# One drain on TensorE raises the chunk semaphore by two, in layer 1 of a two-layer GNN kernel

## The reference

```python
# layer 0
agg = segment_sum((x @ W_l.T + b_l)[src], dst) ; deg = segment_sum(1, dst)
x = layernorm(x + agg / max(deg, 1) + x @ W_r.T)
# layer 1 (reads the edges the other way round: h[dst] summed at src)
neigh = segment_sum(h[dst] @ W_neigh.T + b_neigh, src) / max(deg, 1)
y = h + relu(h @ W_self.T + b_self + neigh)
x = layernorm(h + layernorm(y) * ln_gamma + ln_beta)
```

## Time and profile before

| | |
|---|---|
| median of 3 runs | 4257.75 us (4251.17 to 4269.38) |
| the profiled execution's own time | 4222.63 us |
| its span | 4220.8 us, 57125 instructions |
| TensorE busy, weight loads | 2795.4 us (66%), 1186.1 us (28%) |
| VectorE busy | 2605.4 us (62%) |
| ScalarE busy | 813.8 us (19%) |
| GpSimd busy | 1896.1 us (45%) |
| DMA, mean over the span | 139 GB/s |

### The profile page before, as it was taken

The page is one execution under the profiler, slowest core; times in us unless marked ns, Lnnn a source line. Parts: engine busy times, 40 slices in busy tenths (PEclk is TensorE's granted clock), DMA queues, the critical chain, the costliest instruction groups (busy, mean ns, idle before and its releaser), DMA issues.

```text
span 4220.8 us, 57125 instructions
## 1 busy us (share of the span) xinstructions
PE 2795.4 (66%) x11308; PEld 1186.1 (28%) x11308; DVE 2605.4 (62%) x6523; ACT 813.8 (19%) x2156; POOL 1896.1 (45%) x2073
## 2 busy tenths in 40 slices
PE   1000088888888888866999655555555555568887
PEld 1000033333333433322554211111111111124443
DVE  3878877777777777754555444444444444448887
ACT  0300044444444444410222000000000000002222
POOL 0600066666666666664000366666666666630000
PEclk9555599999999999976999766666566665669999
DMA  3300066666666666664333566666666666661111
GB/s 141 123 0 0 21 169 165 170 165 167 167 169 166 168 167 167 168 202 137 102 103 98 160 178 173 179 179 179 177 178 174 180 177 177 172 115 60 55 60 50
DMA packets 201222, 586.38 MB, mean 139 GB/s; under 512 B 34672, under 2 KB 35502, under 8 KB 201196
## 3 DMA queue, kind: packets, MB, share of 16 engines
q0 software_dynamic: 148480, 488.56, 42.6%
q1 hardware_dynamic: 52716, 97.53, 7.1%
HBM read 534.51 MB, written 51.44 MB: 139 GB/s over the span
## 4 chain that ended last, share of the span: by engine, by line
PE 38%; DVE 19%; issue 19%; DMA 8%; DVEq 6%; POOL 2%; another core or an unknown queue 2%; ACT 2%; SPq 2%; POOLq 0%; ACTq 0%
PE ps L710 37%; DMA rows<-table,idx_ring 7%; DVEq L576 4%; DVE acc L583 3%; DVE onehot L569 2%; POOL rows L364 2%; DVE flat L501 2%; DVE flat L502 1%; DVE flat L503 1%; DVE where L598 1%; PE ps L812 1%; DVE st L658 1%; DVE spot L596 1%; PE ps L815 1%
## 5 line engine op out<-in xcount | busy, mean ns | idle before, releaser
L364 POOL DMA_INDIRECT rows<-table,idx_ring x1856 | 1793.8, 966 | 1394.7 <-issue 462.6
L710 PE MATMUL ps<-rows,onehot 128*128 128x512 f16 (+1 forms) x5568 | 1393.7, 381 | 758.0 <-DVE onehot L569 346.3
L583 DVE TENSOR_TENSOR acc<-acc,ps 128x513 f32 x928 | 638.2, 688 | 830.5 <-issue 353.7
L710 PE MATMUL ps<-where,put 128*128 128x464 f16 x3328 | 805.5, 365 | 348.8 <-ACT put L859 291.4
L710 PEld LDWEIGHTS ps<-rows,onehot 128*128 128x128 bf16 x5568 | 526.5, 111 | 1650.1 <-issue 888.2
L569 DVE TENSOR_SCALAR onehot<-iota_node,loc_ring,rows 128x128 bf16<-128x128 f16 x1856 | 586.4, 323 | 297.6 <-DMA rows<-table,idx_ring 253.1
L858 ACT ACTIVATE put<-spot,flat 128x128 f16<-128x128 f16 x832 | 334.1, 402 | 1091.7 <-DVE spot L596 860.7
L710 PEld LDWEIGHTS ps<-where,put 128*128 128x128 f16 x3328 | 268.1, 98 | 659.2 <-issue 351.8
L598 DVE TENSOR_SCALAR where<-iota_chunk,hi_ring 128x928 f16<-128x928 f16 x832 | 378.8, 455 | 0.0
L872 ACT ACTIVATE flat<-acc,rdeg 128x512 f32 (+1 forms) x98 | 69.4, 710 | 1551.2 <-DVE rdeg L647 1547.6
L710 PE MATMUL ps<-w_a,flat 128*128 128x512 f32 x784 | 356.0, 597 | 0.1
(11 more groups left out here) (131 smaller groups left out, 1361.9 us busy)
## 6 DMA issues: line engine op xcount, KB each, us to landing
rows<-table,idx_ring POOLq DMA_INDIRECT x1856
table<-rows SPq DMA_DIRECT2D x98, 257.0 KB, 3.2
h_scratch<-rows SPq DMA_DIRECT2D x49, 256.0 KB, 2.0
rows<-h_scratch SPq DMA_DIRECT2D x49, 256.0 KB, 2.7
acc<-in_x SPq DMA_DIRECT2D x4, 3072.0 KB, 23.5
rows<-in_x SPq DMA_DIRECT2D x48, 256.0 KB, 3.2
out<-rows SPq DMA_DIRECT2D x48, 256.0 KB, 2.0
w_a<-in_w_l_t SPq DMA_DIRECT2D x1, 1024.0 KB
```

The lines of the kernel that those rows point to most:

```text
L364: nc.gpsimd.indirect_dma_start(out=rows[:, k % GB, :], out_offset=None, in_=tables[layer][:, :], in_offset=bass.IndirectOffsetOnAxis(ap=id ...
L583: V.tensor_tensor(tile_acc, tile_acc, part, ALU.add).then_inc(s_acc, 1)
L710: return nc.tensor.matmul(*args, skip_group_check=True, **kw)
```

## The change

In layer 1 the count product no longer raises the semaphore. After the last product of each group of two chunks, a drain on TensorE raises `s_mm` by two. Layer 0 keeps its raise by one in each chunk. All waits for `s_mm` stay as they are written.

```diff
-                    mm(ps[:, bank + 1, 0:1], lhs, row[:, 2 * D + 2:2 * D + 4].bitcast(bf16)[:, 0:1],
-                       start=start, stop=stop).then_inc(s_mm, 1)
+                    last = mm(ps[:, bank + 1, 0:1], lhs, row[:, 2 * D + 2:2 * D + 4].bitcast(bf16)[:, 0:1],
+                              start=start, stop=stop)
+                    if layer == 0:
+                        last.then_inc(s_mm, 1)
+                    elif stop:
+                        nc.tensor.drain().then_inc(s_mm, g)
```

## The result

The change costs little: 4272.07 us median (4268.03 to 4278.99) against 4257.34 us for the kernel before (4251.17 to 4269.38), a ratio of 1.0035 (1.0025 to 1.0044). That is 15 us of loss (11 to 19), inside what the prediction called the same, and twice its 7.

A forecast was written before the change was run, and what follows sets the result against it. GpSimd's gathers, at 1.25 us each plus stalls, were taken to set layer 1's pace. Credit 7, drain 0 and raises 0 sum to +7 us, put on the 4257.75 us median: 4265 us, range 4215 to 4330.

The forecast's parts named there:

- The term of the credit: Layer 1's gather ring: odd gathers wait for one chunk more, so half the stalls come one gather earlier; +7 us.
- The cases of 0: Layer 1's stalls: a run of gathers that ends sooner starts the next with less lead, so the price is 0.
- the 14 or the 70: Layer 1's early stops: 14 us if 119 stalls replace 112; upper bound 70 us if stalls keep their end.
- I take 0: TensorE's drains in layer 1: hidden in its 585 us of idle time, so 0 us are added.
- The second rival: Layer 1's drain on TensorE is not hidden and delays the next gather's credit: +63 us, 4321 us; chance 13%.
- The size of one uncovered drain: TensorE in layer 1: 0.17 us of a chunk's uncovered end plus 0.24 us of refill, 0.41 us per drain.
- the 190 us: TensorE's time for 464 drains at 0.41 us each in layer 1, forecast to lie in its idle time.
- the gathers that end a stall: Sign in layer 1's gathers on GpSimd: the one ending a stall would nearly always be odd, counted from 1.
- the broken stream: Sign on TensorE in layer 1: its stream of chunks is broken after each pair, at 0.3 to 0.5 us.
- GpSimd's mean long idle: Sign in layer 1: GpSimd's mean idle in long stalls stays as before, with a few more stalls.
- The third rival: Layer 1's drained raise passes where the matmul's is late, giving longer gather runs: 59 us less, 4199 us; chance 15%.
- The first: Layer 1's slow stretches end by themselves, so each early stop is paid in full: +70 us, 4328 us; chance 15%.

## Why the prediction was right, and where it was not

**Time and sign** were right: 4272 in 4215 to 4330, a loss within 0.5%. The number came out partly by luck, since the 7 us stood on the wrong term. **The term of the credit** was too large, 7 us where 1 and 3 were measured (the intervals reach from -2 to 7). Its counting was right: before the padded end, 93 of 97 stalls of the kernel with pairs and no drain stand in front of an odd gather, against 44 of 91 before. What was too dear is what an early stop costs. The cases of 0 (an early stop is made up for) describe it better than the 14 or the 70.

**The step that failed is "I take 0" for the drain**, "It lies in TensorE's idle time". 464 drains cost 14 to 19 us by themselves, and with the credit's 1 to 3 they make the change's 15, within the intervals. The second rival, "the drain is not hidden", is the one that happened, at a quarter of its price of 63 us, and by its own sign: "many new idles of 0.4 to 1 us in mid-run". The size of one uncovered drain was right (0.47 us measured on a backlog, 0.41 worked out). 15 us is 8% of the 190 us that the drains would cost if all stood on the path.

The mistake in the reasoning was to set the drain against idle time as an average. Much of TensorE's idle time lies in the slow stretches (before, 62 idles above 2.5 us hold 241 of the 585) and not in the backlogs behind them, and there an uncovered drain has nothing to hide in. Each takes most of the lead that TensorE gains on the gathers (0.28 us per pair left of 0.75), so that the credit of the next gathers comes a little late. The short idles in the table fit this in size and place; it is read from profiles, and no run tested it by itself.

The other reading is that the holds of 4.7 us cost the time. They are real: idle times of TensorE above 2.5 us in which VectorE completed two one-hots or more occur in none of the kernels without a drain, and 62 times in the first 1290 us of the stage with the drain alone. But TensorE stood still in slow stretches before as well, GpSimd's long idles did not grow, and the kernel with a drain in each chunk has only 4 such holds and loses most. So the holds are not needed for the loss. That they have no part in it with one drain per group is not shown.

Of the other signs, the gathers that end a stall (147 of 155 odd before the padded end) and the broken stream came as forecast. GpSimd's mean long idle did not stay (1.40 us for 1.9), TensorE's idle time in the stage grew from 585 to 621 us, and the stage's 1409.8 us and layer 0's 1460 can't be compared with the profile before.

**The third rival**, that a drained raise passes where a product's is late, is refuted: the drain ends late itself, GpSimd waited for it as long as it had for products, and no kernel with drains is faster than before. **The first** (stalls that keep their end) is refuted by the kernel with six buffers, 9 us where 2.5 us more for each of 112 stalls would have given 280. The inference that a stall ends 0.6 us after the last rows have landed holds in the price and not in the gaps: after the change the restart at 3157.16 comes 3.47 us after the last gather's start and not 4.1.

**On the pages.** The Trainium skill ("PSUM — Partial Sum Buffer", section "Engine vs sequencer instructions") puts the increment on the producing product for correctness, and says that a drain waits until the engine is fully idle. It gives no price. A drain's row here runs until its group's products are over and at times beyond (by 4.7 us in the one shown), and TensorE starts nothing before it ends, which agrees with the second. The runs add the price: raises by two cost 1 us on the product, and 15 with the drain.

The 12 us that 464 fewer increments would save by the Trainium skill ("TensorE: Matmul & The Clock Gate", section "The cost: per-tile semaphore tail") did not show: the two kernels of layer 1 that differ in that alone measured 1.0003 and 1.0007, 2 us apart with intervals of 4 us either way.

**Open.** What the slow stretches are: the runs show their marks (register instructions of 0.70 us, products' signals and drains that end late), and that they are absent in the one set that ran on the fastest chip. The 434 to 465 us between that chip and the others are most likely their cost. Whether it is the chip or its state at the time can't be told from one set each. What the change costs on a chip without them was not tried, nor a product's length added to each group at an unchanged clock, which would settle how much of the cost is the backlog.

## What to carry to other kernels

Put a raise of a whole group on the group's last product, where its cost could not be told from nothing in layer 1, and keep drains off a stream that others feed: each drain uncovers the end of a product and a refill. Don't cover a cost with an engine's average idle time; ask whether the idle lies at the moments when the cost falls. An engine that is idle for over 40% of a stage can still need its full pace in the backlog behind a stall. When a loss is small, sort the waits of the engine that sets the pace by length: here the long ones held nearly everything and did not change, and the short ones held the loss. And before two profiles are subtracted, compare a stretch that the change cannot touch: here layer 0 alone differed by more than the whole effect.

## What the runs showed of the hardware

- The same kernel has medians of 4253, 4222 and 3787 us on three chips, each steady there within 0.5%, single disturbed executions apart. Between the profiles of 4222.63 us (before) and 3794.63 us (pairs in both layers), 412 of the 428 us lie in the two stretches with indirect gathers.
- A drain on GpSimd behind indirect gathers took 4.36 us at the median, one on TensorE 1.81 us with the products that it waits for, and at times 6.4.
- A drain between two groups of six products on TensorE, at the lower clock (the six in 1.92 us, where other groups took 1.07), took 0.47 us: 2.22 us from group to group where 1.75 were in the stream.
- One product more per group raised TensorE's granted clock from 0.62 to 0.76 of full speed, and a drain in each chunk lowered it to 0.50, the lower of its two levels (1.2 GHz) for the whole of that stretch.
